# Delta attention: block products in pairs, redrawn queues, and an opening block with four buffers

## The reference

```python
q = _l2norm(_short_conv(x @ Wq, conv_q)) * d ** (-0.5)      # causal convolution, 4 taps, then silu
k = _l2norm(_short_conv(x @ Wk, conv_k)); v = _short_conv(x @ Wv, conv_v)
def step(S, inp):
    qt, kt, vt, bt, gt = inp
    S = S * jnp.exp(gt)[..., None, None]
    for i in range(nh):
        ki, vi, bi = kt[:, :, i], vt[:, :, i], bt[:, :, i]
        kS = jnp.einsum('bhd,bhde->bhe', ki, S)
        S = S + bi[..., None, None] * (ki[..., None] * (vi - kS)[:, :, None, :])
    return S, jnp.einsum('bhd,bhde->bhe', qt, S)
```

## Time and profile before

| | |
|---|---|
| median of 3 runs | 3219.11 us (3215.27 to 3219.3) |
| the profiled execution | 3221.68 us |
| its span, first to last instruction | 3219.9 us |
| mean granted TensorE clock | 0.959 |
| busy, share of span: TensorE, VectorE, ScalarE, GpSimd | 93 %, 79 %, 70 %, 61 % |

### The profile page before, as it was taken

One profiled execution on the slowest core, in us unless ns is written; L12 is line 12 of the kernel. 1 busy time (PEld: TensorE's weight loads), 2 busy tenths in 40 slices (PEclk: granted clock), 3 DMA queues, 4 the chain that ended last, 5 costly groups with the idle time before them and its releaser, 6 DMA issues. The chain is left out here.

```text
span 3219.9 us, 83441 instructions
## 1 busy us (share of the span) xinstructions
PE 3008.8 (93%) x27212; PEld 2368.3 (74%) x27212; DVE 2537.5 (79%) x5859; ACT 2250.6 (70%) x6953; POOL 1972.9 (61%) x3125
## 2 busy tenths in 40 slices
PE   5569999999999999999999999999987999767999
PEld 3458888888888888888888888888876444455444
DVE  5669999999999999999999999999754454594554
ACT  4768888888888888888888888888643343412443
POOL 1588888888888888888888888888831000100000
PEclk8779999999999999999999999999998899967999
DMA  4457777676777667676767677777532333002322
GB/s 102 122 143 172 180 190 178 172 180 169 179 178 188 179 175 179 174 175 176 187 176 182 173 176 179 175 178 184 151 93 74 148 123 124 10 3 76 145 116 112
DMA packets 588204, 482.87 MB, mean 150 GB/s; under 512 B 464784, under 2 KB 504368, under 8 KB 581632
## 3 DMA queue, kind: packets, MB, share of 16 engines
q1 hardware_dynamic: 583552, 475.44, 55.3%
q10 hardware_dynamic: 4224, 2.10, 0.2%
HBM read 285.53 MB, written 191.86 MB: 148 GB/s over the span
## 5 line engine op out<-in xcount | busy, mean ns | idle before, releaser
L919 DVE SCALAR_TENSOR_TENSOR conv_k<-PP,tk,conv_k 128x256 f32<-128x256 f32 x1536 | 722.6, 479 | 61.0 <-ACT conv_k L754 33.3
L692 POOL TENSOR_TENSOR X<-X,tmp 96x31 f32<-96x31 f32 (+15 forms) x992 | 534.5, 539 | 77.8
L919 DVE SCALAR_TENSOR_TENSOR conv_v<-PP,tv,conv_v 128x256 f32<-128x256 f32 x1152 | 539.3, 477 | 45.0 <-ACT conv_v L754 35.3
L689 POOL TENSOR_TENSOR tmp<-At,X 96x31 f32<-96x31 f32 (+15 forms) x992 | 486.6, 491 | 63.6 <-DMA At<-n_d 5.4
L1088 PE MATMUL PP<-xn,wk 128*128 128x268 f32 x1024 | 342.7, 419 | 35.3 <-DVE conv_k L919 26.5
L675 POOL TENSOR_TENSOR rk<-ss,half 96x8 f32<-96x8 f32 x128 | 209.1, 1633 | 175.4 <-DVE ss L887 175.4
L657 POOL TENSOR_TENSOR Sg<-S,gend 128x512 f32<-128x512 f32 x256 | 266.1, 1040 | 63.3 <-DVE S L878 63.3
L726 ACT ACTIVATE recA<-TG,es 96x128 f32<-96x128 f32 x1024 | 284.8, 368 | 6.0 <-DVE es L912 6.0
L754 ACT ACTIVATE conv_k<-PP,tk 128x256 f32<-128x256 f32 x512 | 245.2, 480 | 56.2 <-PE PP L1088 49.0
L718 ACT ACTIVATE recA<-TG 128x128 f32<-128x128 f32 x1024 | 265.5, 272 | 24.5 <-PE TG L1139 24.5
L1052 PE MATMUL RB<-rhs,Yf 96*96 96x128 f32 x2048 | 269.1, 274 | 14.5 <-DVE rhs L867 14.3
(11 more groups left out here) (289 smaller groups left out, 6776.1 us busy)
## 6 DMA issues: line engine op xcount, KB each, us to landing
kqg_d<-kqgA SPq DMA_DIRECT2D x128, 512.0 KB, 6.2
kqgB<-kqg_d SPq DMA_DIRECT2D x128, 512.0 KB, 4.3
rec_d<-recA SPq DMA_DIRECT2D x128, 480.0 KB, 3.4
recB<-rec_d SPq DMA_DIRECT2D x128, 480.0 KB, 5.6
f1gates<-f1gates_d SPq DMA_DIRECT2D x24, 1024.0 KB, 6.7
f2gates<-f2gates_d SPq DMA_DIRECT2D x24, 1024.0 KB, 6.8
gdec<-gdec_d SPq DMA_DIRECT2D x128, 128.0 KB, 5.6
apk_d<-apkA SPq DMA_DIRECT2D x128, 128.0 KB, 3.3
```

The costliest lines, as they stand in the source:

```text
L689: nc.gpsimd.tensor_tensor(t, At[q % 2][:, j, j + 1:].unsqueeze(2).broadcast_to(sh), X[q % 2][:, j, 0:cols].unsqueeze(1).broadcast_to(sh), ...
L692: nc.gpsimd.tensor_tensor(x, x, t, ALU.subtract).then_inc(sub_ev, 1)
L919: return nc.vector.scalar_tensor_tensor(acc, src[:, :, j:j + SPAN], w[:, j:j + 1], acc, ALU.mult, ALU.add)
```

## The change

1. `zm`: the units of the second half lie on rows 64 to 127 of `apkB`, `Dd` and `ZW`, and the products alternate between the halves. `apkB` is loaded in two transfers instead of one, `Dd` in four instead of two, `zev` makes four copies instead of two.
2. `ss_` adds the constant from a tensor (`g.tiny`, set once by GpSimd) instead of as an immediate.
3. The order of calls of every engine in the loop is new, and the loop is turned so that most calls use f-1 where they used f.
4. The opening block: `gm` has four buffers; another order of `raw`, `hat`, `gates`, of `square`, `keep_x`, `keep_xn`, and of `centre`, `var_eps`, `norm`; the table's fourth transfer of each head is issued by ScalarE.

```diff
-        gm = sb("gm", [128, 2, NC, TC])
+        DEEP = 4
+        gm = sb("gm", [128, DEEP, NC, TC])
@@ prologue, tensor
             raw(0)
             raw(1)
+            raw(2)
             hat(0)
-            raw(2)
+            raw(3)
             pe.wait_ge(w_in, 16 * 7)
             hat(1)
             gates(0)
-            raw(3)
             hat(2)
             gates(1)
+            gates(2)
             hat(3)
-            gates(2)
             gates(3)
@@ prologue, scalar
             for q in range(B):
+                square(q)
                 keep_x(q)
-                square(q)
-                if q:
-                    keep_xn(q - 1)
+                if q >= 2:
+                    keep_xn(q - 2)
+            keep_xn(B - 2)
             keep_xn(B - 1)
...
 +                if h:
+                    act.wait_ge(mask_ev, h)
+                    keep_table(nc.scalar, h - 1, B - 1)
+            act.wait_ge(mask_ev, NH)
+            keep_table(nc.scalar, NH - 1, B - 1)
@@ prologue, vector
-                var_eps(q - 1)
                 centre(q)
-                norm(q - 1)
+                var_eps(q - 1)
+                if q >= 2:
+                    norm(q - 2)
...
-            sums(0)
-            sums(1)
+            for h in range(DEEP - 1):
+                sums(h)
@@ delta_attention
-        apkB, Dd = two("apkB", [64, U, 64]), two("Dd", [64, U, 64])
+        apkB, Dd = two("apkB", [128, HU, 64]), two("Dd", [128, HU, 64])
...
-                sp.dma_start(apkB[N % 2][:, :, :], apk_d[slot(N)]).then_inc(ld_da[N % 2], 16)
+                for hf in range(2):
+                    sp.dma_start(apkB[N % 2][64 * hf:64 * hf + 64, :, :], half(apk_d[slot(N)], hf)).then_inc(ld_da[N % 2], 16)
...
-                nc.scalar.activation(Zt[32:64, :, 0:32], ZW[0:32, :, 0:32], ACT.Copy, scale=-1.0)
-                nc.scalar.activation(Zt[64:96, :, :], ZW[32:64, :, :], ACT.Copy, scale=-1.0).then_inc(zev_ev, 1)
+                for hf in range(2):
+                    nc.scalar.activation(half(Zt, hf)[32:64, :, 0:32], ZW[64 * hf:64 * hf + 32, 0:HU, 0:32], ACT.Copy, scale=-1.0)
+                    last = nc.scalar.activation(half(Zt, hf)[64:96, :, :], ZW[64 * hf + 32:64 * hf + 64, 0:HU, :], ACT.Copy, scale=-1.0)
+                last.then_inc(zev_ev, 1)
...
-                nc.vector.tensor_scalar(ss[:, :], ksum[:, :], 1e-6, None, ALU.add).then_inc(ss_ev, 1)
+                nc.vector.tensor_tensor(ss[:, :], ksum[:, :], g.tiny[:, :], ALU.add).then_inc(ss_ev, 1)
...
-                for u in range(U):
-                    last = mm(ZW[0:64, u, :], apkB[N % 2][:, u, :], Dd[N % 2][:, u, :], start=True, stop=True)
+                for u in range(HU):
+                    for hf in range(2):
+                        o = slice(64 * hf, 64 * hf + 64)
+                        last = mm(ZW[o, u, :], apkB[N % 2][o, u, :], Dd[N % 2][o, u, :], start=True, stop=True)
```

More of the change, by code:

```diff
@@ L155, in _ @@
                 sp.wait_ge(mask_ev, h + 1)
-                for b in range(B):
-                    sp.dma_start(g.edec_d[h, :, :, b, :], ex[TC * b:TC * (b + 1), h, :].rearrange("t (s x) -> t s x", x=SPAN)).then_inc(g.edec_out[h], 16)
+                for b in range(B - 1):
+                    keep_table(sp, h, b)
             sp.wait_ge(g.gdec_out, 16 * NH)
@@ L208, in _ @@
                 for a in range(2):
-                    last = nc.tensor.matmul(GE[h % 2][:, a, :], after_bd[:, :], gm[:, h % 2, 16 * a:16 * (a + 1), :], start=True, stop=True)
+                    last = nc.tensor.matmul(GE[h % 2][:, a, :], after_bd[:, :], gm[:, h % DEEP, 16 * a:16 * (a + 1), :], start=True, stop=True)
                 last.then_inc(ge_mm, 1)
@@ L256, in _ @@
             nc.gpsimd.memset(g.half[:, :], 0.5)
+            nc.gpsimd.memset(g.tiny[:, :], 1e-6)
             nc.gpsimd.memset(g.minus_half[:, :], -0.5).then_inc(preset, 1)
@@ L698, in _ @@
                 r, c = f - BACK - 1, f - BACK
-                x_zero(*group_at(f, 3))
-                fo_(r - 1)
-                kqg(f - 1)
-                sg(r, 0)
-                rk_(f - 1)
-                subst(*group_at(f, GROUP + 1), range(0, 6))
-                sg(r, 1)
-                subst(*group_at(f, GROUP + 1), range(6, 12))
+                sg(r - 1, 0)
+                kqg(f - 2)
+                rk_(f - 2)
+                subst(*group_at(f - 1, GROUP + 1), range(0, 5))
+                sg(r - 1, 1)
+                subst(*group_at(f - 1, GROUP + 1), range(5, 7))
+                fo_(r - 1)
+                x_zero(*group_at(f - 1, 3))
+                subst(*group_at(f - 1, GROUP + 1), range(7, 12))
         @block.scalar
@@ L832, in _ @@
                 r, c = f - BACK - 1, f - BACK
-                xt(*group_at(f, 2 * GROUP + 1))
-                tap0(c, "v0")
-                tap0(c, "v1")
-                ksum_(f - 1, 1)
-                ksum_(f - 1, 0)
-                wev(r, 0)
-                tap0(c, "v2")
-                gate_(c)
-                zev(c)
-                tap0(f, "k1")
-                mo_(r, 0)
-                tap0(f, "k0")
-                kr(f - 1, 0)
-                vsilu(c)
-                kr(f - 1, 1)
-                tap0(f, "k2")
-                w12(c)
-                wev(r, 1)
-                q2_(f - 1)
-                tap0(f, "q")
-                mo_(r, 1)
-                yev(c)
-                ksilu(f)
-                qsilu(f)
+                tap0(c - 1, "v0")
+                tap0(c - 1, "v1")
+                ksum_(f - 2, 1)
+                ksum_(f - 2, 0)
+                wev(r - 1, 0)
+                tap0(c - 1, "v2")
+                xt(*group_at(f - 1, 2 * GROUP + 1))
+                gate_(c - 1)
+                zev(c - 1)
+                tap0(f - 1, "k1")
+                tap0(f - 1, "k0")
+                kr(f - 2, 0)
+                kr(f - 2, 1)
+                w12(c - 1)
+                vsilu(c - 1)
+                mo_(r - 1, 0)
+                tap0(f - 1, "k2")
+                q2_(f - 2)
+                tap0(f - 1, "q")
+                wev(r - 1, 1)
+                yev(c - 1)
+                ksilu(f - 1)
+                qsilu(f - 1)
+                mo_(r - 1, 1)
         @block.vector
@@ L987, in _ @@
                 r, c = f - BACK - 1, f - BACK
[L988 to L1023 removed]
+                tap1(c - 1, "v0")
+                tap2(c - 1, "v0")
+                osb_(r - 2)
+                rhs_(r - 1, 0)
+                tap1(c - 1, "v1")
+                tap3(c - 1, "v0")
+                tap2(c - 1, "v1")
+                og_(r - 2)
+                tap3(c - 1, "v1")
+                ss_(f - 2)
+                rinv_(f - 2)
+                step_(f - 2)
+                acc_(r - 2)
+                tap1(c - 1, "v2")
+                tap2(c - 1, "v2")
+                tap3(c - 1, "v2")
+                es_(f - 2)
+                sup(r - 1, 0)
+                tap1(f - 1, "k1")
+                tap1(f - 1, "k0")
+                tap2(f - 1, "k1")
+                tap2(f - 1, "k0")
+                tap3(f - 1, "k0")
+                tap3(f - 1, "k1")
+                rhs_(r - 1, 1)
+                ap(f - 2, 0)
+                ap(f - 2, 1)
+                tap1(f - 1, "k2")
+                tap2(f - 1, "k2")
+                tap1(f - 1, "q")
+                tap3(f - 1, "k2")
+                tap2(f - 1, "q")
+                tap3(f - 1, "q")
+                vr(c - 1, 0)
+                vr(c - 1, 1)
+                sup(r - 1, 1)
         @block.tensor
@@ L1205, in _ @@
                 r, c = f - BACK - 1, f - BACK
+                zm(c - 1)
+                ot(r - 2)
+                w_(r - 1, 0)
+                v_tile(c - 1, 2)
+                out(r - 2)
+                gate_tile(c - 1)
+                sr(r - 1, 0)
+                o_(r - 1, 0)
+                k_tile(f - 1, 1)
+                k_tile(f - 1, 0)
+                wm(c - 1)
+                ks(r - 1, 1)
+                gram(f - 2, 0)
+                gram(f - 2, 1)
+                k_tile(f - 1, 2)
+                k_tile(f - 1, 3)
+                w_(r - 1, 1)
+                m3(c - 1)
+                vtr(c - 1, 1)
+                vtr(c - 1, 0)
+                o_(r - 1, 1)
+                sr(r - 1, 1)
                 v_tile(c, 0)
```

99 lines of the change are left out of this document (24 added, 75 removed).

## The result

The changed kernel takes 3568.1 us (median of 4 runs, 3554.3 to 3578.9) against 3219.2 beside it (4 runs); the ratio is 1.108, 95 % interval 1.106 to 1.110. Its span is 3559.8 us at a mean granted clock of 0.934.

A forecast was written before the change was run, and what follows sets the result against it. TensorE was taken as the bound. Full stretch -9.3, opening -5.5 and -2.4, filling -3, emptying -4 sum to -24.2 us: 3197.5 from the profiled 3221.7, 3195 against the median; 8-in-10 range 3169 to 3226.

The forecast's parts named there:

- The new order of the queues: All engines' redrawn queues in the loop: claimed 0 stalls in a plain step, bounds 0 and +0.2 us.
- the stall of the transposition: Rival: ScalarE's `xt` costs 2.0 us instead of 0.83 every fourth step, +36 us, 3231; chance 0.13, shared with similar stalls.
- The constant: VectorE's `ss` with a tensor addition: between 0 and twice its 162 ns, VectorE not the bound, so 0.
- Paired products: TensorE's `zm` on two diagonal quarters side by side: -0.45 us a step, bounds 0 and -0.5.
- The rival in which the pairs do not overlap: `zm` stays at 1.07 us and the fifth narrow stay is pure loss: +58 us, 3253; chance 0.09.
- One more change of tile shape: TensorE gets five narrow-shape stays a step instead of four: +0.35 us a step, bounds 0.2 and 0.45.
- The step with the transposition: Every fourth step, with `xt` just ahead of ScalarE's gate: 0.83 us longer instead of 0.75, bounds 0 and 2.0.
- The two extra ScalarE copies: `zev` in four copies on ScalarE: +0.3 us a step, hidden in its idle time.
- The six loads: Six loads instead of three: about 1.6 us more of the SP queue a step, hidden in SP's waits.
- Opening block: Before the loop: stores end at 72 instead of 77.49 us, -5.5; gates partly before the last transposition, -2.4.
- Filling: Pipeline start: K squares go ahead of `xt`, so step scales are ready when it ends: -3 us, bounds 0 and -6.
- Emptying: Steps without K work at the end: wait before `o1` covered, fifth narrow stay paid: -4 us, bounds 0 and -10.

## Why the prediction was wrong

*The step that failed is "The new order of the queues"*: "I take 0 stalls in a plain step, bounds 0 and +0.2". The steps that start between 400 and 2200 us rose by 3.05 us in the mean (17.71 to 20.76). I had laid the GpSimd order out in time, with `fo`, five substitution steps and `Sg` in a row, and checked that each result was there for its reader. I did not ask what runs beside them on VectorE. The rows to ask it of were in the trace of before, in the filling. VectorE, then GpSimd:

```profile
207.77 1.66 DVE L887 TENSOR_SCALAR ss<-ksum 128x8 f32<-128x8 f32 x1 [3.88 <-ACT recA L718]
```
```profile
207.14 1.58 POOL L642 TENSOR_TENSOR kqgA<-kq,gdec 128x768 f32<-128x768 f32 x1
208.67 0.73 POOL L643 TENSOR_TENSOR kqgA<-kq,gdec 128x256 f32<-128x256 f32 x1
```
This `ss` lasts ten times that of the earlier trace rows, after its wait of 3.88 us, and ends at 209.43, when the second `kqgA` does (209.40): the whole mechanism in three rows. None of my rivals had this mechanism; the stall of the transposition, the nearest, was priced at 36 us where 347 came. The range ended at 3226. Nor had the prediction a term for the clock: it read 1.00 in the stretch before and let it stand, while the waits brought 226 us at 1.2 GHz with them.

*"The constant"*, 0: right, 1.0004 when it is added alone. *"Paired products"*, -0.45: right, 1.07 to 0.62 us in one bank of the accumulators. The rival in which the pairs do not overlap is out, and the rule on one bank that I had set beside it (the Trainium skill, TensorEngine Tiling (Array Packing), Gotcha 1: PSUM Pressure) didn't show here as time: by it `zm` would have stayed at 1.07. *"One more change of tile shape"*, +0.35: 17.40 with it against 17.10 in the kernel with the pairs alone, +0.30, though these two differ in all their queues; with `m3` alone moved, 0.24 in the rows around it. *The plain step*, 17.42: 17.40 once GpSimd is out of the way. *The step with the transposition*, +0.83: +0.94. The group, -0.32: 3 x 17.40 + 18.34 = 70.54, -0.29. *"The two extra ScalarE copies"* and *"The six loads"*, hidden: the kernel with the pairs alone has them too, and its plain step fell by 0.42.

*"Opening block"*, -5.5 and -2.4: -5.3 to the first `zm` when alone. The last gates end at 32.85 instead of 38.68, 5.8 earlier, not 2.4, and the last mask at 64.3 instead of 73.99; but the 24 stores take 0.87 us each, not the 0.69 of the earlier trace rows, so they end at 70.72 and bound the block. Each term was off, the sum by 2.6. *"Filling"*, -3: `ss` of that step starts 0.19 us after `xt` starts, as forecast, but the next one is held 2.62 us (before: 1.66). From the last store to the first `zm` it is 140.1 us in the changed kernel and 141.9 with GpSimd's old order, against 141.6 before: -1.5 and +0.3, not -3. *"Emptying"*, -4 (the product -0.33 x 11 gives -3.6): with GpSimd's old order the last 12 distances between `zm` sum to 190.4 instead of 194.9, -4.5, and 0.8 are lost behind them.

Together these terms give -20.7 in the trace of the kernel with GpSimd's old order, where the prediction had -24.2: first `zm` -7.4, in between -14.1, behind +0.8. The sum was nearly right for that kernel and had no term for the one thing that decided. There the full stretch gave -9.6 where -9.3 was forecast, and the ends -11.1 where -14.9 was.

## What to carry to other kernels

When an order is redrawn, lay the queues of VectorE and GpSimd side by side, and look at what runs at the same time, not only at who waits for whom: a 0.15 us instruction of VectorE that falls on a block of GpSimd reads lasts as long as the block. The sign in a profile is an instruction whose mean duration is many times that of its like and whose end falls together with the end of GpSimd's; no wait is shown for it. Put GpSimd's gapless reads ahead of the short instructions with room to spare; behind something that waits for the first of them, they met the next ones here, and 110 us of the loss stayed. When a wait of some 2 us is added to every step, look at the granted clock too: here it added 90 to 100 us to the 250 of the waits.
